# A vision tower with three attention experts on one Trainium2 core: the third expert's images shared out over both partition halves

## The chip, the cores and the metric

The kernel runs on one core of a Trainium2 chip. The time is device microseconds of one execution. It is measured without a profile; beside it one execution was profiled, and its trace is what is read below.

## The reference

16 images of 3 x 96 x 96 are cut into 36 patches each (6 x 6 of 16 x 16), so there are 576 tokens of 192 features. All arrays are float32.

```python
h = patches @ Wp.T + bp                                   # (16, 36, 768) -> (16, 36, 192)
a = window_attention(h)                                   # 12 heads of 64, window 65, zero padded
h = layernorm(h + a @ w_out + b_out)
gate = softmax(relu(h @ Wg1 + bg1) @ Wg2 + bg2)           # three experts, the two best kept
q, k = split(h @ Wqk + bqk)                               # three heads of 64, one per expert
for e in range(3):
    v = h @ Wv[e] + bv[e]
    # e == 0: q goes through a depthwise convolution of width 3 over the tokens
    # e == 1: global keys that the causal mask hides; e == 2: a position bias is added
    y[e] = causal_softmax(q[e] @ k[e].T / 8) @ v
h = layernorm(h + concat(w[e] * y[e]) @ Wp + bp)          # w: softmax over the two best gates
```

## The kernel before, in words

The images form two groups (g = 0, 1) of eight, 288 tokens each. Activations lie with the features on the partitions and the 288 tokens of a group as columns. Almost every product is made in the format float32r from a high and a low part, so that one projection is five matmuls; scores, probabilities and transposes are plain float32.

The attention runs over 16 **entries**, numbered 0 to 15: entries 0 to 5 are the six pairs of heads of group 0, 6 to 11 those of group 1, 12 and 13 the two pairs of experts of group 0, 14 and 15 those of group 1. In an entry the first head lies on partitions 0 to 63 and the second on 64 to 127. Entries 12 and 14 hold experts 0 and 1. Entries 13 and 15 hold expert 2 alone, and before the change it stands in both halves: its columns of the weights are laid out twice, and both halves compute the same for all eight images.

The work is cut into **steps**, and one list for each engine (`PE_ORDER`, `ACT_ORDER`, `DVE_ORDER`) gives their order by hand. Engines wait for one another by semaphores alone, so a step that waits holds up all that stands behind it in its list. The steps of entry n, in the order of the data:

- `qk n` (PE, L814 to L839): query and key, ten matmuls of 288 columns into two of three `proj` banks; `cq n` (ACT, L432 to L457): two copies to SBUF, three for entries 12 and 14, whose query also goes to `cn n` (DVE, L710 to L721), the convolution. The banks go round in the order of the list, and `take` makes PE wait until the bank's last user is read (`freed_by`).
- `s n` (PE, L886 to L916): the mask goes into the score bank by one matmul (L902; float32 with the position bias for entries 13 and 15, bf16 for the others), then 16 small products of 64 rows and 36 columns, one per image and half (L913). A small float32 matmul gives two records in the trace.
- `sh n` (DVE, L628 to L637): row maximum and subtraction; `ex n` (ACT, L466 to L469): exponential; `nm n` (DVE, L639 to L657): sum, reciprocal, gate's weight for entries 12 to 15, product.
- `t n` (PE, L918 to L925): three transposes, for image tiles of three, three and two images; `sp n` (ACT, L471 to L479): three copies, each with a scale of ones and zeros per partition, which spread the blocks so that images don't mix; `pv n` (PE, L927 to L946): probabilities by values, twelve records; `oh n`, `ol n` (ACT L481 to L485, DVE L659 to L663): high and low part of the output.

Around these: `xs`, `em` (splitting and embedding the patches), `wq`, `wv`, `wo`, `wf` (splitting weights; `wf 0` is the copy `ffn_hi` at L423), `v g j` and `cv g j` (values of attention), `outa`, `outb g t` (residual and output projection of a token tile), `st`, `rs`, `ap g t` (statistics on DVE, inverse deviation on ACT, normalising on DVE), `tr g` (back to features), `h1 g` (high and low part). Then the experts: `gate g` (L864 to L875), `cg g`, `lg g` (L877 to L884: sixteen products of three columns, one per image and half, at L883), `gd g` (DVE, L722 to L753: 17 small instructions), `ge g` (ACT, L522 to L528: two exponentials in the middle of `gd`, each waiting for DVE), `fv g z` and `cf g z` (experts' values), `res2`, `one2`, `out2 g t` (residual, experts 0 and 1, expert 2), `st2`, `rs2`, `ap2 g t`, `tr2 g`, `fin g` and the store. The gate's weights lie in `wgt`, per half, group, pair and image. POOL makes the low parts of weights, after a few memsets (L354 to L363).

## Time and profile before

| | us |
|---|---|
| median of the runs shown | 121.96 |
| lowest run | 121.11 |
| the profiled execution | 121.46 |
| its span, first to last instruction | 119.7 |

Three runs were timed: 121.11, 121.96 and 561.58, of which the last is an outlier. PE executes the matmuls, PEld loads their weights, DVE is the vector engine, ACT the scalar engine, POOL the third of these and SP issues the DMAs. A row of the chain that ended last has start, duration, what it was, and how many instructions were put together; a matmul's duration there is the time until the next one takes over. A row of a timeline has start, duration, engine, line, operation, operands with their shapes, and in brackets how long the engine was idle before it and what ended that. L883 is line 883. Some tiles share memory: `wqk_f` also holds the gate's values and the normalised tokens, `tw_hi` and `tw_lo` the experts' outputs, `tw_f` the result, `x_hi` and `x_lo` the attention's outputs. `g_t` and `fg_w` are `g1_t` and `fg2_w`.

### The profile page before, as it was taken

What the parts mean: (1) busy time and instruction counts of PE and PEld (TensorE: products, weight loads), DVE (VectorE), ACT (ScalarE), POOL (GpSimd) and SP (SyncE); (2) the same over time, 40 slices, a digit from 0 to 9 for tenths busy, and PEclk for the clock granted to TensorE, in tenths of its full rate; (3) what the DMA queues carried; (4) which work ended last, traced back from release to release, by engine and by line L of the source; (5) the groups of instructions that cost most, each with busy time, mean ns of one, the idle gap of its engine ahead of it and who ended that gap; (6) DMA issues with size and microseconds to landing.
All of it is one profiled execution on the core that took longest, in us unless ns stands there. A gap on an engine that the chain in (4) does not pass through costs nothing.

```text
span 119.7 us, 3567 instructions
## 1 busy us (share of the span) xinstructions
PE 109.4 (91%) x1411; PEld 97.0 (81%) x1411; DVE 76.8 (64%) x232; ACT 71.4 (60%) x196; POOL 21.5 (18%) x32
## 2 busy tenths in 40 slices
PE   6979999999999999999999899999868999897940
PEld 4769998987799888889998899899767898795930
DVE  0467848730582844593876776876847678998581
ACT  4469855459938758654458666652364485447450
POOL 6003614471400910000007900000000000000000
PEclk9999999999999999999999999999999999999998
DMA  3999999100000000000000000000000000000102
GB/s 92 255 362 404 416 424 398 43 0 5 3 0 5 3 0 0 5 0 5 0 5 0 0 0 5 0 5 0 0 3 0 8 0 5 0 5 0 54 20 74
DMA packets 3675, 7.80 MB, mean 65 GB/s; under 512 B 844, under 2 KB 1996, under 8 KB 3532
## 3 DMA queue, kind: packets, MB, share of 16 engines
q1 hardware_dynamic: 3660, 7.59, 17.6%
q8 instruction: 11, 0.18, 0.6%
q14 instruction: 4, 0.03, 0.1%
HBM read 7.14 MB, written 0.44 MB: 63 GB/s over the span
## 4 chain that ended last, share of the span: by engine, by line
PE 66%; DVE 16%; ACT 5%; issue 5%; DMA 4%; SPq 2%; DVEq 0%; ACTq 0%
PE proj L846 10%; PE score L913 8%; PE outp L944 6%; PE outp L813 4%; PE proj L831 4%; DMA x_f<-x_t 4%; PE trans L923 4%; PE proj L835 3%; PE proj L832 3%; PE score L813 3%; PE proj L838 3%; PE proj L839 3%; PE score L902 2%; PE proj L969 2%; DVE ln_st L670 2%
## 5 line engine op out<-in xcount | busy, mean ns | idle before, releaser
L478 ACT ACTIVATE pt_t<-trans,image_t 108x216 f32<-108x216 f32 (+1 forms) x48 | 16.5, 419 | 2.3 <-PE trans L923 2.3
L469 ACT ACTIVATE score<-d_t 128x296 f32<-128x296 f32 (+1 forms) x16 | 6.7, 418 | 10.8 <-DVE d_t L635 10.7
L913 PEld LDWEIGHTS score<-k_t,q_t 64*36 64x36 f32 x480 | 10.3, 111 | 3.1 <-issue 1.4
L913 PE MATMUL score<-k_t,q_t 64*36 64x37 f32 (+1 forms) x480 | 12.1, 196 | 0.1
L644 DVE TENSOR_REDUCE sm_t<-score 128x8 f32<-128x288 f32 x16 | 7.2, 449 | 7.6 <-ACT score L469 7.5
L632 DVE TENSOR_REDUCE mx_t<-score 128x8 f32<-128x296 f32 (+1 forms) x16 | 7.3, 456 | 4.5 <-PE score L913 4.4
L969 PE MATMUL proj<-wo_hi,x_hi 128*108 128x192 f32 (+1 forms) x36 | 9.5, 264 | 0.0
L971 PE MATMUL proj<-wo_lo,x_hi 128*108 128x192 f32 (+1 forms) x36 | 9.2, 256 | 0.0
L974 PE MATMUL proj<-wo_hi,x_lo 128*108 128x192 f32 (+1 forms) x36 | 9.2, 256 | 0.0
L444 ACT ACTIVATE q_t<-proj 128x288 f32<-128x288 f32 x12 | 4.9, 410 | 6.5 <-PE proj L839 6.3
L499 ACT ACTIVATE ln_ln<-ln_mv,const 108x1 f32<-108x1 f32 (+1 forms) x12 | 3.5, 294 | 8.6 <-DVE ln_mv L673 8.6
L846 PE MATMUL proj<-wv_hi,h_hi 128*108 128x384 f32 (+1 forms) x24 | 8.3, 346 | 0.0
L923 PE MATMUL trans<-const,p_t 128*108 128x128 f32 (+1 forms) x48 | 8.2, 280 | 0.0
L831 PE MATMUL proj<-h_hi,wqk_hi 128*128 128x288 f32 x24 | 7.6, 332 | 0.4 <-DVE h_lo L694 0.3
L655 DVE TENSOR_TENSOR p_t<-score,sm_t 128x288 f32<-128x288 f32 x16 | 7.3, 458 | 0.8 <-DVE sm_t L648 0.3
L635 DVE TENSOR_TENSOR d_t<-score,mx_t 128x296 f32<-128x296 f32 (+1 forms) x16 | 7.4, 464 | 0.5
L584 DVE TENSOR_TENSOR x_lo<-x_f,x_hi 128x288 fp32r<-128x288 f32 x12 | 6.1, 518 | 2.6 <-ACT x_hi L407 2.6
L485 ACT ACTIVATE x_hi<-outp 128x288 fp32r<-128x288 f32 x12 | 4.9, 409 | 4.7 <-PE outp L944 4.6
L367 POOL TENSOR_TENSOR wqk_lo<-wqk_f,wqk_hi 128x256 fp32r<-128x256 f32 x6 | 4.6, 772 | 17.1 <-ACT wqk_hi L411 17.0
L838 PE MATMUL proj<-h_lo,wqk_hi 128*128 128x288 f32 x24 | 6.7, 296 | 0.0
L839 PE MATMUL proj<-h_lo,wqk_hi 128*128 128x288 f32 x24 | 6.7, 294 | 0.0
L832 PE MATMUL proj<-h_hi,wqk_lo 128*128 128x288 f32 x24 | 6.7, 295 | 0.0
(170 smaller groups left out, 331.2 us busy)
## 6 DMA issues: line engine op xcount, KB each, us to landing
ffn_f<-f_w SPq DMA_DIRECT2D x1, 1088.0 KB, 12.6
wqk_f<-w_qk SPq DMA_DIRECT2D x2, 512.0 KB, 8.1
x_f<-x_t SPq DMA_DIRECT2D x2, 432.0 KB, 5.7
wv_f<-w_v SPq DMA_DIRECT2D x1, 768.0 KB, 6.9
wo_f<-w_out SPq DMA_DIRECT2D x1, 768.0 KB, 9.7
x_f<-x_t SPq DMA_DIRECT2D x2, 288.0 KB, 4.7
tw_f<-tok_w SPq DMA_DIRECT2D x2, 256.0 KB, 4.4
wqk_f<-w_qk SPq DMA_DIRECT2D x2, 256.0 KB, 5.0
```

The source lines that it names most:

```text
L478: nc.scalar.activation(pt_t[:, n % 2, 0:tiles, :, i], trans[0:ROWS, 0:tiles, :, 0:TOK], ACT.Copy, scale=image_t[:, i:i + 1]).then_inc(spli ...
L813: ins = nc.tensor.matmul(embed_bank[g][m][:, 0:GT], a[:, k, cols], b[:, g, k], start=(k == 0 and z == 0), stop=(k == PK - 1 and z == 2))
L831: nc.tensor.matmul(b, w_hi[:, 0, c], hcols(h_hi, g, 0), start=True, stop=False)
L832: nc.tensor.matmul(b, w_lo[:, c], hcols(h_hi, g, 0), start=False, stop=False)
L838: nc.tensor.matmul(b, w_hi[:, 0, c], hcols(h_lo, g, 0), start=False, stop=False)
L839: nc.tensor.matmul(b, w_hi[:, 1, c], hcols(h_lo, g, 1), start=False, stop=True).then_inc(projected, 1)
L846: ins = nc.tensor.matmul(out, htile(h, c, g, j), w, start=(n == 0), stop=(n == len(ops) - 1))
L913: ins = nc.tensor.matmul(s[64 * h:64 * h + TOK, im, 0:width], q, k_t[rows, n % QK_RING, im, 0:width], start=False, stop=True, skip_group_c ...
L923: ins = nc.tensor.transpose(trans[0:tile_rows(j), j].rearrange("p h s -> p (h s)"), p_t[:, n % 2, tile_cols(j)], ident)
L969: nc.tensor.matmul(b[0:rows, 0:DIM], o_hi[:, g, p, cols], wo_hi[:, p, 0:DIM], start=False, stop=False, skip_group_check=True)
L971: nc.tensor.matmul(b[0:rows, 0:DIM], o_hi[:, g, p, cols], wo_lo[:, p, 0:DIM], start=False, stop=False, skip_group_check=True)
L974: return nc.tensor.matmul(b[0:rows, 0:DIM], o_lo[:, g, p, cols], wo_hi[:, p, 0:DIM], start=False, stop=(p == PAIRS - 1), skip_group_check= ...
```

## The change

For entries 13 and 15 (`halved`) query and key now come from one projection: 128 columns of the weights, 64 of the query and 64 of the key, five matmuls into one bank. The two copies bring both to partitions 0 to 63. The eight images are shared out over the halves of the score bank in five slots: images 0 to 2 and 6 to the first half, 3 to 5 and 7 to the second, with two half-slots left empty. Maximum, exponential, sum and product run over five slots. There are two transposes, and four copies that bring the blocks to where the products with the values read them; both halves of those products read the same block. The gate's logits are computed for eight slots as before and for these five, thirteen in all; the two empty half-slots have weights of zero and a bias of -1e30 for expert 2 (`no_w`), so that their weight is zero. All three lists are ordered anew. In the diff "..." stands for what is left out: only the new arguments by which the same functions take the number of slots, and the tiles' declarations.

```diff
+HALF_SLOTS = 5
+GATES = GI + HALF_SLOTS
...
+LAST = ("ffn", 1)
+
+
+def halved(n):
+
+    return ENTRIES[n][0::2] == LAST
+
+
+def half_image(h, i):
+
+    return 3 * h + i if i < 3 else 6 + h if i == 3 + h else None
+
+
+def splits_through(n):
+
+    return sum(4 if halved(m) else 3 for m in range(n + 1))
...
 PE_ORDER = """
-em 0, em 1, em 2, em 3, em 4, em 5, em 6, qk 0, em 7, em 8, em 9, qk 1, s 0, v 0 0, s 1, em 10, em 11
-v 0 1, t 0, qk 2, v 0 2, s 2, t 1, qk 3, rows 0, s 3, pv 0, qk 4, v 1 0, t 2, qk 5, pv 1, s 4, v 1 1, pv 2
-s 5, v 1 2, t 3, qk 6, pv 3, t 4, qk 7, s 6, t 5, pv 4, s 7, qk 8, pv 5, outa 0 0, outb 0 0, t 6, s 8
-outa 0 1, outb 0 1, outa 0 2, outb 0 2, pv 6, qk 9, t 7, tr 0, s 9, qk 10, t 8, pv 7, s 10, gate 0, t 9
-qk 11, fv 0 0, s 11, t 10, pv 8, pv 9, fv 0 1, lg 0, pv 10, t 11, outa 1 0, pv 11, outa 1 1, outb 1 0
-outb 1 1, outa 1 2, outb 1 2, qk 12, tr 1, s 12, qk 13, gate 1, s 13, t 12, qk 14, lg 1, pv 12, t 13
-fv 1 0, qk 15, pv 13, s 14, s 15, fv 1 1, res2 0 0, one2 0 0, out2 0 0, res2 0 1, one2 0 1, out2 0 1, t 14
-res2 0 2, one2 0 2, out2 0 2, pv 14, t 15, tr2 0, res2 1 0, pv 15, res2 1 1, one2 1 0, one2 1 1, out2 1 0
+em 0, em 1, em 2, em 3, em 4, em 5, em 6, qk 0, em 7, s 0, qk 1, em 8, em 9, em 10, s 1, v 0 0, qk 2
+em 11, s 2, t 0, v 0 1, v 0 2, t 1, qk 3, pv 0, rows 0, s 3, t 2, qk 4, v 1 0, s 4, qk 5, v 1 1, t 3, pv 1
+s 5, pv 2, pv 3, t 4, qk 6, pv 4, qk 7, v 1 2, s 6, s 7, t 5, qk 8, pv 5, outa 0 0, s 8, outb 0 0, t 6
+outa 0 1, outb 0 1, outa 0 2, outb 0 2, qk 9, t 7, pv 6, tr 0, s 9, qk 10, pv 7, t 8, s 10, gate 0, qk 11
+t 9, pv 8, fv 0 0, pv 9, s 11, fv 0 1, t 10, lg 0, pv 10, t 11, outa 1 0, pv 11, outa 1 1, outb 1 0
+outb 1 1, outa 1 2, outb 1 2, qk 12, tr 1, s 12, qk 13, gate 1, s 13, t 12, lg 1, pv 12, qk 14, t 13
+qk 15, fv 1 0, pv 13, s 14, fv 1 1, s 15, res2 0 0, res2 0 1, one2 0 0, out2 0 0, one2 0 1, t 14, res2 0 2
+one2 0 2, out2 0 1, out2 0 2, pv 14, t 15, tr2 0, pv 15, res2 1 0, res2 1 1, one2 1 0, out2 1 0, one2 1 1
 out2 1 1, res2 1 2, one2 1 2, out2 1 2, tr2 1
 """
 ACT_ORDER = """
-xs 0, xs 1, xs 2, xs 3, xs 4, xs 5, wq 0, xs 6, xs 7, xs 8, hh 0, wq 1, xs 9, xs 10, cq 0, wv 0, cq 1
-xs 11, wq 2, ex 0, ex 1, cv 0 0, wq 3, wq 4, cv 0 1, cq 2, sp 0, cv 0 2, hh 1, wq 5, sp 1, cq 3, ex 2
-br 0, cq 4, oh 0, cv 1 0, wo 0, ex 3, oh 1, cq 5, sp 2, oh 2, ex 4, cv 1 1, cv 1 2, sp 3, cq 6, ex 5, sp 4
-oh 3, cq 7, ex 6, oh 4, sp 5, cq 8, ex 7, oh 5, sp 6, rs 0 0, rs 0 1, wf 0, rs 0 2, ex 8, cq 9, oh 6, h1 0
-sp 7, cq 10, ex 9, sp 8, cg 0, sp 9, ex 10, oh 7, cq 11, oh 8, ex 11, sp 10, oh 9, oh 10, sp 11, ge 0
-oh 11, rs 1 0, rs 1 1, rs 1 2, cq 12, h1 1, ex 12, cq 13, cg 1, ex 13, sp 12, cq 14, ge 1, sp 13, oh 12
-oh 13, cq 15, ex 14, ex 15, rs2 0 0, sp 14, rs2 0 1, rs2 0 2, sp 15, fin 0, oh 14, oh 15, rs2 1 0, rs2 1 1
-rs2 1 2, fin 1
+xs 0, xs 1, xs 2, xs 3, xs 4, xs 5, wq 0, xs 6, xs 7, xs 8, hh 0, xs 9, wq 1, xs 10, cq 0, wv 0, cq 1
+xs 11, wq 2, ex 0, wq 3, wq 4, cv 0 0, cq 2, hh 1, wq 5, wo 0, ex 1, cv 0 1, sp 0, cv 0 2, ex 2, sp 1
+cq 3, br 0, cq 4, sp 2, ex 3, cv 1 0, oh 0, cq 5, ex 4, cv 1 1, oh 1, sp 3, ex 5, oh 2, sp 4, cq 6, oh 3
+cq 7, cv 1 2, ex 6, sp 5, cq 8, oh 4, oh 5, ex 7, wf 0, sp 6, ex 8, rs 0 0, rs 0 1, rs 0 2, cq 9, h1 0
+oh 6, sp 7, cq 10, ex 9, oh 7, sp 8, cg 0, ex 10, cq 11, sp 9, oh 8, oh 9, ex 11, sp 10, oh 10, sp 11
+ge 0, oh 11, rs 1 0, rs 1 1, rs 1 2, cq 12, h1 1, ex 12, cq 13, cg 1, ex 13, sp 12, ge 1, cq 14, sp 13
+oh 12, oh 13, cq 15, ex 14, ex 15, sp 14, rs2 0 0, rs2 0 1, rs2 0 2, sp 15, oh 14, fin 0, oh 15, rs2 1 0
+rs2 1 1, rs2 1 2, fin 1
 """
 DVE_ORDER = """
-xs 0, xs 1, xs 2, xs 3, xs 4, xs 5, xs 6, hl 0, xs 7, xs 8, xs 9, wv 0, im 0, xs 10, sh 0, xs 11, sh 1
-nm 0, nm 1, hl 1, sh 2, br 0, pm 0, nm 2, sh 3, ol 0, nm 3, ol 1, sh 4, sh 5, ol 2, nm 4, nm 5, sh 6, ol 3
-nm 6, ol 4, sh 7, ol 5, st 0 0, nm 7, ap 0 0, st 0 1, sh 8, ap 0 1, st 0 2, ap 0 2, nm 8, h1 0, ol 6, sh 9
-nm 9, sh 10, nm 10, ol 7, cf 0 0, sh 11, ol 8, nm 11, cf 0 1, ol 9, ol 10, gd 0, ol 11, st 1 0, st 1 1
-ap 1 0, ap 1 1, st 1 2, ap 1 2, cn 12, h1 1, sh 12, nm 12, sh 13, nm 13, gd 1, cn 14, ol 12, ol 13, sh 14
-cf 1 0, nm 14, sh 15, st2 0 0, cf 1 1, st2 0 1, nm 15, st2 0 2, ap2 0 0, ap2 0 1, ap2 0 2, ol 14, fin 0
-ol 15, st2 1 0, st2 1 1, st2 1 2, ap2 1 0, ap2 1 1, ap2 1 2, fin 1
+xs 0, xs 1, xs 2, xs 3, xs 4, xs 5, xs 6, xs 7, hl 0, xs 8, xs 9, im 0, xs 10, sh 0, wv 0, nm 0, xs 11
+sh 1, hl 1, nm 1, sh 2, nm 2, sh 3, br 0, nm 3, sh 4, ol 0, nm 4, ol 1, sh 5, pm 0, ol 2, ol 3, nm 5, sh 6
+nm 6, ol 4, sh 7, ol 5, sh 8, nm 7, st 0 0, st 0 1, ap 0 0, ap 0 1, st 0 2, ap 0 2, nm 8, h1 0, ol 6, sh 9
+nm 9, ol 7, sh 10, nm 10, ol 8, cf 0 0, ol 9, sh 11, nm 11, cf 0 1, ol 10, gd 0, ol 11, st 1 0, st 1 1
+ap 1 0, ap 1 1, st 1 2, ap 1 2, cn 12, h1 1, sh 12, nm 12, sh 13, nm 13, gd 1, cn 14, cf 1 0, ol 12, ol 13
+sh 14, cf 1 1, sh 15, nm 14, st2 0 0, nm 15, st2 0 1, st2 0 2, ap2 0 0, ap2 0 1, ap2 0 2, fin 0, ol 14
+ol 15, st2 1 0, st2 1 1, ap2 1 0, st2 1 2, ap2 1 1, ap2 1 2, fin 1
 """
...
-            if kind == "qk":
+            if kind == "qk" and halved(key):
+                plan("q", key, (k_s, key + 1))
+            elif kind == "qk":
                 plan("q", key, (q_s, key + 1) if ENTRIES[key][0::2] != ("ffn", 0) else (taps_s, ENTRIES[key][1] + 1))
                 plan("k", key, (k_s, key + 1))
...
+            pool.memset(no_w[:], 0.0).then_inc(zeroed, 1)
+            pool.wait_ge(zeroed, 6)
+            pool.memset(no_w[32:33, 2:3], NEG).then_inc(zeroed, 1)
...
+                if halved(n):
+                    both, col = bank("q", n)[:, 0:GT], B_QK + 2 * p
+                    nc.scalar.activation(q_t[0:HD, n % QK_RING], both[0:HD], ACT.Identity,
+                                         bias=bias[0:HD, col:col + 1]).then_inc(q_s, 1)
+                    nc.scalar.activation(k_t[0:HD, n % QK_RING, :, 0:TOK], by_image(both[HD:128]), ACT.Identity,
+                                         bias=bias[HD:128, col + 1:col + 2]).then_inc(k_s, 1)
+                    return
...
-                    if p == 0:
-                        act.wait_ge(conv_b_s, 2)
-                        if g:
-                            act.wait_ge(scored, ENTRY_OF[("ffn", 0, 0)] + 1)
-                        nc.scalar.activation(qc_t[:], by_image(q[0:HD]), ACT.Identity, bias=conv_b[:],
-                                             scale=bias[0:HD, B_CONVW + 1:B_CONVW + 2]).then_inc(taps_s, 1)
+                    act.wait_ge(conv_b_s, 2)
+                    if g:
+                        act.wait_ge(scored, ENTRY_OF[("ffn", 0, 0)] + 1)
+                    nc.scalar.activation(qc_t[:], by_image(q[0:HD]), ACT.Identity, bias=conv_b[:],
+                                         scale=bias[0:HD, B_CONVW + 1:B_CONVW + 2]).then_inc(taps_s, 1)
...
+                if halved(n):
+                    for i in range(3):
+                        nc.scalar.activation(pt_t[:, n % 2, 0:2, 0, i], trans[0:ROWS, 0, :, 0:TOK], ACT.Copy,
+                                             scale=image_t[:, i:i + 1]).then_inc(split, 1)
+                    nc.scalar.activation(pt_t[0:2 * TOK, n % 2, 2, 0, 0:2], trans[0:2 * TOK, 1, :, 0:TOK],
+                                         ACT.Copy).then_inc(split, 1)
+                    return
...
-                nc.vector.tensor_tensor(d_t[:, n % 2, :, 0:width], s[:, :, 0:width],
-                                        mx_t[:, n].unsqueeze(2).broadcast_to([128, GI, width]),
+                nc.vector.tensor_tensor(d_t[:, n % 2, 0:slots, 0:width], s[:, :, 0:width],
+                                        mx_t[:, n, 0:slots].unsqueeze(2).broadcast_to([128, slots, width]),
...
-                    link(nc.vector.tensor_tensor(sm_t[:, n, 2], sm_t[:, n, 1], wgt[:, g, p], ALU.mult))
+                    link(nc.vector.tensor_tensor(share, inverse, wgt_last[:, g] if halved(n) else wgt[:, g], ALU.mult))
...
-                nc.vector.tensor_tensor(by_image(p_t[:, n % 2]), e[:, :, 0:TOK],
-                                        sm_t[:, n, 2].unsqueeze(2).broadcast_to([128, GI, TOK]),
+                nc.vector.tensor_tensor(by_image(p_t[:, n % 2, 0:slots * TOK]), e[:, :, 0:TOK],
+                                        share.unsqueeze(2).broadcast_to([128, slots, TOK]),
...
-                wide = lambda z: z.unsqueeze(2).broadcast_to([128, GI, 3])
+                wide = lambda z: z.unsqueeze(2).broadcast_to([128, GATES, 3])
                 dve.wait_ge(projected, ready[("lg", g)])
-                lg = bank("lg", g)[:, 0:3 * GI].rearrange("p (i e) -> p i e", e=3)
+                lg = bank("lg", g)[:, 0:3 * GATES].rearrange("p (i e) -> p i e", e=3)
...
+                nc.vector.tensor_tensor(wgt[0:64, g], kept[0:64, 0:GI, 0], s[4][0:64, 0:GI], ALU.mult).then_inc(gated, 1)
+                nc.vector.tensor_tensor(wgt[64:128, g], kept[64:128, 0:GI, 1], s[4][64:128, 0:GI],
+                                        ALU.mult).then_inc(gated, 1)
+                nc.vector.tensor_tensor(wgt_last[:, g], kept[:, GI:GATES, 2], s[4][:, GI:GATES],
+                                        ALU.mult).then_inc(gated, 1)
...
-                banks = [take(name, n)[:, 0:GT] for name in "qk"]
-                cols = (slice(0, 128), slice(128, 256))
+                if halved(n):
+                    banks, cols = [take("q", n)[:, 0:GT]], (slice(HD, HD + 128),)
+                else:
+                    banks = [take(name, n)[:, 0:GT] for name in "qk"]
+                    cols = (slice(0, 128), slice(128, 256))
...
+                for i in range(HALF_SLOTS):
+                    for h in range(2):
+                        im = half_image(h, i)
+                        ins = nc.tensor.matmul(b[SLOT * h:SLOT * h + SLOT, 3 * (GI + i):3 * (GI + i) + 3],
+                                               g1_t[:, im or 0], fg2_w[:] if im is not None else no_w[:],
+                                               start=True, stop=True)
                 ins.then_inc(projected, 1)
...
-                nc.tensor.matmul(s[:, :, 0:width], idn, mask.unsqueeze(1).broadcast_to([128, GI, width]), start=True,
+                nc.tensor.matmul(s[:, :, 0:width], idn, mask.unsqueeze(1).broadcast_to([128, slots, width]), start=True,
...
+                if halved(n):
+                    for i in range(HALF_SLOTS):
+                        for h in range(2):
+                            im = half_image(h, i)
+                            if im is not None:
+                                ins = nc.tensor.matmul(s[64 * h:64 * h + TOK, i, 0:width],
+                                                       q_t[0:HD, n % QK_RING, TOK * im:TOK * im + TOK],
+                                                       k_t[0:HD, n % QK_RING, im, 0:width],
+                                                       start=False, stop=True, skip_group_check=True)
+                    ins.then_inc(scored, 1)
+                    return
...
+                    pe.wait_ge(split, splits_through(n - 1))
                 pe.wait_ge(normed, n + 1)
+                if halved(n):
+                    for j, blocks in enumerate((slice(0, 3), slice(3, 5))):
+                        rows = TOK * (blocks.stop - blocks.start)
+                        ins = nc.tensor.transpose(trans[0:rows, j].rearrange("p h s -> p (h s)"),
+                                                  p_t[:, n % 2, TOK * blocks.start:TOK * blocks.stop], ident)
+                    ins.then_inc(transposed, 1)
+                    return
...
-                pe.wait_ge(split, 3 * n + 3)
+                pe.wait_ge(split, splits_through(n))
...
-                        probs = pt_t[0:rows, n % 2, j, h].rearrange("p i t -> p (i t)")[:, 0:rows]
+                        probs = pt_t[0:rows, n % 2, j, 0 if halved(n) else h].rearrange("p i t -> p (i t)")[:, 0:rows]
```

## Rows read from the trace of the kernel before

**Rows 1.** The page: busy us, share of span, instructions by engine

```profile
PE 109.4 (91%) x1411; PEld 97.0 (81%) x1411; DVE 76.8 (64%) x232; ACT 71.4 (60%) x196; POOL 21.5 (18%) x32
```

**Rows 2.** Stretches: us, busy by engine (instructions), PE clock, DMA share, GB/s

```profile
8.60:86.50 77.90, 76.97 (x1014) 69.48 (x1014) 50.53 (x149) 50.38 (x137) 19.53 (x20) 1.00 0.17 68
86.50:119.70 33.20, 25.64 (x364) 22.36 (x364) 23.37 (x77) 16.63 (x51) 0.00 (x0) 0.99 0.05 15
...
97.36:110.46 13.10, 11.71 (x170) 9.96 (x171) 11.69 (x44) 7.25 (x25) 0.00 (x0) 1.00 0.01 3
```

**Rows 3.** DVE's timeline behind 92 us

```profile
94.52 0.46 DVE L632 TENSOR_REDUCE mx_t<-score 128x8 f32<-128x288 f32 x1 [0.54 <-PE score L913]
...
97.36 0.18 DVE L729 TENSOR_REDUCE wqk_f<-proj 128x8 f32<-128x24 f32 x1
...
100.68 0.50 DVE L717 SCALAR_TENSOR_TENSOR qc_t<-q_t,bias,qc_t 64x280 f32<-64x280 f32 x1
...
102.65 0.46 DVE L632 TENSOR_REDUCE mx_t<-score 128x8 f32<-128x288 f32 x1 [0.20 <-PE score L913]
...
103.52 0.55 DVE L706 TENSOR_TENSOR wv_f<-proj,bv_all 108x384 f32<-108x384 f32 x1
...
109.23 1.23 DVE L685 TENSOR_SCALAR wqk_f<-proj,ln_mv,ln_rs 108x192 f32<-108x192 f32 x3
...
116.56 0.45 DVE L699 COPY tw_f<-proj 64x288 f32<-64x288 f32 x1 [0.44 <-PE proj L1013]
```

**Rows 4.** Chain that ended last: start us, us, what

```profile
56.98 0.33 PE trans L923 x3
...
61.66 1.91 ACT ffn_hi L423
...
76.83 1.03 PE proj L883 x32
...
92.65 0.66 PE proj L874 x5
93.31 0.49 PE score L902 x2
93.80 0.70 PE score L913 x32
...
101.86 0.77 PE score L913 x23
...
111.31 0.65 PE outp L944 x12
```

**Rows 5.** Groups by form: busy us, mean ns, idle before

```profile
L478 ACT ACTIVATE pt_t<-trans,image_t 108x216 f32<-108x216 f32 x32 | 12.2, 436 | 2.3 <-PE trans L923 2.3
...
L478 ACT ACTIVATE pt_t<-trans,image_t 108x144 f32<-108x144 f32 x16 | 6.2, 385 | 0.0
...
L685 DVE TENSOR_SCALAR wqk_f<-proj,ln_mv,ln_rs 108x192 f32<-108x192 f32 x8 | 3.6, 467 | 0.1
...
L687 DVE TENSOR_SCALAR wqk_f<-proj,ln_mv,ln_rs 108x64 f32<-108x64 f32 x4 | 1.3, 332 | 0.0
```

**Rows 6.** PE's timeline at the start of `qk 10`

```profile
66.76 0.37 PE L831 MATMUL proj<-h_hi,wqk_hi 128*128 128x288 f32 x1 [0.31 <-DVE h_lo L694]
```

**Rows 7.** ACT's timeline behind 86 us

```profile
92.89 0.49 ACT L457 ACTIVATE k_t<-proj,bias 128x288 f32<-128x288 f32 x1
...
96.77 0.51 ACT L449 ACTIVATE q_t<-proj,bias 128x288 f32<-128x288 f32 x1
...
97.62 0.50 ACT L457 ACTIVATE k_t<-proj,bias 128x288 f32<-128x288 f32 x1
...
99.14 0.22 ACT L527 ACTIVATE wqk_f<-wqk_f 128x24 f32<-128x24 f32 x1 [0.91 <-DVE wqk_f L741]
...
109.78 1.01 ACT L478 ACTIVATE pt_t<-trans,image_t 108x216 f32<-108x216 f32 x3
...
112.00 0.41 ACT L485 ACTIVATE tw_hi<-outp 128x288 fp32r<-128x288 f32 x1 [0.45 <-PE outp L944]
```

39 lines of the change are left out of this document (19 added, 20 removed).

## Prediction

> **What bounds the kernel now.** I read the page's busy shares first, then busy time by stretches, then the chain that ended last, then each engine's own timeline where the chain changes engine. PE is busy for 109.4 of 119.7 us [rows 1]. Cut at 86.5 us (where `outb 1 2`, the last matmul of group 1's attention, is done), the two parts differ. Up to there PE is busy 76.97 of 77.90 us, at full clock: what is added to PE or taken from it counts in full. After it PE is busy only 25.64 of 33.20 us; between 97.36 and 110.46 DVE is busy 11.69 of 13.10 us, and the end hangs on DVE's list [rows 2]. DVE's last copy, `fin 1`, ends at 116.56 + 0.45 = 117.0 [rows 3]; the 2.7 us from there to 119.7 are the output's way to memory. The profiled run took 121.46 us around its span of 119.7, so 1.8 us lie outside. I sum against that run. The median shown is 121.96 and the lowest 121.11, so it stands between them.
>
> **Prices on PE.** Five projection matmuls of 288 columns take 0.66 us [rows 4]. A full projection of query and key has ten, the halved one five: 0.66 us less. The mask matmul of this entry is float32 over 288 columns and takes 0.49 us, in two passes [rows 4]; over 5 x 36 = 180 columns it takes 0.49 x 180/288 = 0.31, so 0.18 less. Scores of 16 products (32 records) take 0.70 us [rows 4]; eight take 0.35, if they still overlap in pairs as now. Three transposes take 0.33 us [rows 4]; one goes, 0.11. Together 1.30 us a group. The logits, 16 products (32 records), take 1.03 us [rows 4]; ten more for the five new slots, the two empty half-slots against `no_w` included, cost 10/16 x 1.03 = 0.64 us. Net 0.66 us less PE work a group, 1.3 in all. But it doesn't fall where it is counted: `lg 0` lies in the part that PE fills, and all halved steps (entries 13 and 15) lie behind 86.5 us. So the first part gets **0.64 us longer**, and the gain has to show in the tail.
>
> The scores of a halved entry take all their operands from the same 64 rows and write to alternate halves. The nearest rows for that are two. The logits do it too, at 1.03 us for 32 records, against 0.70 for the scores [rows 4]: eight products then cost 0.52 us. The products with the values (L944) also alternate halves over one range of rows, twelve records of up to 108 columns in 0.65 us, 54 ns each [rows 4]; by the mask's 0.85 ns a column and pass (0.49/576) 108 columns alone take 92, so those pairs do overlap. Bounds 0.35 and 0.52; I take 0.35, since the logits move only three columns and must be held by something else. The Trainium skill (TensorE: Matmul & The Clock Gate, "The mechanism") says that weight loads overlap matmuls in flight only when their row groups differ; by that rule pairing would gain next to nothing and each halved entry would end 0.17 us later. The logits' row speaks for it, L944 against it.
>
> **Prices on DVE and ACT.** On DVE 192 elements take 467 ns and 64 take 332: 1.05 ns an element [rows 5]. Maximum, subtraction, sum and product go from 288 to 180 elements, 4 x 108 x 1.05 ns = 0.45 us less for each of entries 13 and 15. `gd 1`, 97.36 to 100.7 now [rows 3], grows by 15 elements in five instructions and by 5 to 10 in the rest: 0.15 us more. On ACT a split takes 436 ns for 216 elements and 385 for 144 [rows 5], so about 335 for 72, and four of these stand where there were three of about 420: no gain and no loss (bounds -0.1 to +0.2). The exponential has 108 elements less, 0.1 us; query and key remain two copies. The new memsets are on POOL, which is busy for 21.5 us of the span [rows 1], at its start: nothing; without that cover some 0.3 us.
>
> **The first part, 8.6 to 86.5.** The new lists have the same matmuls in another order, so what can be won is what PE loses now. `qk 10` starts at 66.76, after a wait of 0.31 for `h1 0` [rows 6] and a step (`s 9`) that was late itself. Behind this is the chain through the statistics of group 0, and in it the copy `wf 0`, 1.91 us of ACT between two inverse deviations [rows 4]. The new list has `wf 0` ahead of `sp 6`, where ACT has time; `rs 0 2` isn't behind it, and `ap 0 2` and `tr 0` come up to 0.9 us sooner. I laid the new lists out by hand over the durations of before, with their waits and proj banks, and got `qk 10` at 65.9. Earlier on `s 0` goes ahead of `em 8`, and `qk`, `v` and `pv` alternate so that a copy is done one step ahead; where one is late (`cv 0 2` for `qk 3`, `sp 0` for `t 1`) it costs under 0.1. Bounds for the reordering: 0 (each stall that goes is replaced) to 1.3. I take 0.85. Against the 0.64 of `lg 0` the attention of group 1 ends 0.2 us earlier.
>
> **The tail, step by step** (on the old clock). `qk 12`, `tr 1`, `s 12` stand as they were. The copies for `s 13` end at 92.89 + 0.49 = 93.38 as before [rows 7], but its mask is long done; the eight products start at 93.45 and `sh 13` at 94.0, straight behind `nm 12`, not at 94.52 [rows 3]: 0.5 won. `sh 13` and `nm 13`, 0.45 shorter, end at 96.3 instead of 97.36. Meanwhile `lg 1` goes ahead of `pv 12` and `qk 14`: from 94.4, 1.03 + 0.64 and the way through the array, ready at 96.25. So `gd 1` starts at 96.3 and ends at 99.8. Behind `qk 14` (1.33 by the row of five) `lg 1` would have set it to 97.6.
>
> Here is a wait with a queue behind it. `ge 1` now stands before `cq 14` on ACT, and its second exponential waits for DVE: it starts at 99.14, 1.8 us after `gd 1` [rows 3, 7]. Behind it stand `cq 14` (96.77 to 98.12, 1.35) and `sp 13` (1.01, as `sp 15`) [rows 7], and for these wait `fv 1 0`, `pv 13`, `s 14`. With G the start of `gd 1`, `cq 14` starts at G + 2.05, `sp 13` ends at G + 4.4, and after `pv 13` (0.65) and the mask the products of `s 14` start at G + 5.35. For G = 96.3 that is 101.65, against 101.86 now [rows 4]: of 1.0 us won 0.2 is left, as ACT is now what `s 14` waits for. DVE uses its slack: `cf 1 0` (0.55) [rows 3] is done ahead of `sh 14`. From `sh 14` (102.4, now 102.65) to the end of the three `ap2 0` (109.23 + 1.23 = 110.46) [rows 3] DVE needs 7.8 - 0.45 (entry 15) - 0.5 (`cf 1 0`) = 6.9: done at 109.3, 1.1 earlier. `st2 0 1` now stands behind `nm 15`, so `t 15` can go at 108. `sp 15` waits for `rs2 0 2` as before, 108.7 instead of 109.78; `pv 15` has no `res2 1 0` before it, and `oh 15` starts at 110.65 instead of 112.00 [rows 7]. From there the end is the old one, with `ap2 1 0` pushed ahead of `st2 1 2`, 0.1 lost: `fin 1` starts at 115.3 instead of 116.56 [rows 3], **1.25 us won** in the tail.
>
> Sum: 121.46 + 0.64 - 0.85 - 1.25 = 120.0. A layout by hand overlooks gaps such as the 0.31 of [rows 6]; with 0.2 for one, **120.2 us**.
>
> **Rivals.**
> 1. *The wait moves, little is left.* ACT's queue (`ge 1`, `cq 14`, `sp 13`) takes the tail's first gain, and new waits in the first part eat the 0.85; 0.7 of the tail remains. For it: `s 14` gains only 0.2 in my own layout. Against it: 0.45 and `cf 1 0` come off the engine that sets the end there. 121.46 + 0.64 - 0.7 = 121.4.
> 2. *More comes off.* All of the 1.3 in the first part, and `s 14` keeps the whole 1.0 because `cq 14` isn't what it waits for: 121.46 + 0.64 - 1.3 - 1.25 - 0.8 = 118.8. For it: PE is idle for 7.6 us behind 86.5 [rows 2]. Against it: the queue on ACT stands in the list.
> 3. *Slower: the gate's wait ahead of `cq 14`.* G decides: up to 96.5 the products of `s 14` start no later than now, and each 0.1 us beyond costs 0.1. If the halved scores and `lg 1` come late, so that `gd 1` starts at 97.4 as now, `s 14` starts at 102.75, 0.9 later, and DVE idles meanwhile. With nothing won in the first part: 121.46 + 0.64 + 0.9 = 123.0. Against it: `lg 1` has been taken ahead of 1.3 us of projection.
> That the change doesn't do what it says I exclude: the counts follow from the lists.
>
> **How the numbers follow.** Forecast (119.5 to 121) 0.52; rival 1 (121 to 122) 0.2; rival 2 (under 119.5) 0.17; rival 3 (over 122) 0.11. 8 in 10: 119.0 to 122.2. A measurement here tells about 2% from no change, and 2% under 121.5 to 122 is 119.1 to 119.5. Faster by over 2%: rival 2, 0.17; slower by over 2% (124 and more): the far end of rival 3, 0.04; within: 0.79.
>
> **What the next profile should show.** Halved scores of 0.35 us (0.52 if pairs don't overlap); logits of 1.67; `outb 1 2` 0.2 us earlier; `gd 1` 1.2 us earlier; an ACT wait before the second gate exponential with `cq 14` behind it; DVE without a gap from `sh 14` to `ap2 0 2`; a span of 118.3 to 118.6. I am wrong if group 1's attention ends later than now, or if the way from there to `fin 1` is less than 0.7 us shorter.

## The result, and the profile after

| | before | after |
|---|---|---|
| median, us | 121.53 (4 runs) | 122.65 (4 runs) |
| lowest | 120.99 | 121.84 |
| profiled execution | 121.46 | 123.23 |
| its span | 119.7 | 121.5 |

The change makes the kernel slower, by 0.9%: ratio 1.0088, 95% interval 1.0045 to 1.0131. Forecast was 120.2 us, 1.3 us less than before; it came out 1.1 more. The ratios here and in the table of the experiments leave out executions more than 1.5% above the fastest of their kernel, most of which have a low clock of TensorE, so the medians, over all executions, have to be read beside them.

First the stretches of the changed kernel, cut where the last matmul of group 1's attention is done (now 87.85), and one more stretch that will matter (columns as in [rows 2]):

```profile
8.60:87.85 79.25, 78.25 (x1034) 70.17 (x1034) 52.26 (x149) 51.53 (x136) 19.44 (x20) 1.00 0.17 66
87.85:121.50 33.65, 25.62 (x340) 22.48 (x340) 23.10 (x77) 16.53 (x53) 0.00 (x0) 0.91 0.05 15
98.40:101.80 3.40, 3.40 (x16) 3.34 (x15) 2.33 (x15) 1.36 (x5) 0.00 (x0) 0.50 0.02 5
```

Against [rows 2] the first part takes 79.25 us instead of 77.90, 1.35 more where 0.2 less was expected, and the second 33.65 instead of 33.20. The last row is new: for 3.4 us TensorE runs at 0.50 of its clock, at 1.2 GHz. In the profile of before the clock was at 1.00 up to 118.9 us.

PE's timeline around the first logits (mask of `s 11`, `lg 0`, `pv 10`) in the kernel before, and under it ACT's (`ex 11`, `sp 10`):

```profile
73.52 0.30 PE L902 MATMUL score<-band,bfc 128*128 128x296 bf16 x1
76.76 1.10 PE L883 MATMUL proj<-fg_w,g_t 33*64 33x3 f32 x32
77.79 0.72 PE L944 MATMUL outp<-pt_t,x_f 108*64 108x108 f32 x12
```

```profile
76.09 0.42 ACT L469 ACTIVATE score<-d_t 128x296 f32<-128x296 f32 x1
76.43 1.03 ACT L478 ACTIVATE pt_t<-trans,image_t 108x216 f32<-108x216 f32 x3
```

The same in the changed kernel:

```profile
75.58 0.30 PE L952 MATMUL score<-band,bfc 128*128 128x296 bf16 x1
77.44 1.10 PE L927 MATMUL proj<-fg_w,g_t 33*64 33x3 f32 x32
78.39 0.55 PE L932 MATMUL proj<-fg_w,g_t 33*64 33x3 f32 x13
...
79.15 0.72 PE L1012 MATMUL outp<-pt_t,x_f 108*64 108x108 f32 x12
```

```profile
77.62 0.42 ACT L500 ACTIVATE score<-d_t 128x296 f32<-128x296 f32 x1 [1.51 <-DVE d_t L673]
77.98 1.03 ACT L516 ACTIVATE pt_t<-trans,image_t 108x216 f32<-108x216 f32 x3
```

Read it backwards. `pv 10` (L944, now L1012) needs the three copies of `sp 10` (L478, now L516). They stand on ACT behind `ex 11` (L469, L500), which waits 1.51 us for DVE; DVE has `sh 11` to do for it, and that needs `s 11`. Before, `s 11`'s mask (L902) starts at 73.52 and `ex 11` at 76.09. The new PE list has `pv 8` and `pv 9` ahead of `s 11`, where they stood behind it: 75.58 and 77.62. From `lg 0` to `pv 10` there are 1.71 us instead of 1.03.

The tail, on DVE (`sh 13`, first of `gd 1`, `sh 14`, three of `ap2 0`, last of `ap2 1`, `fin 1`):

```profile
95.53 0.35 DVE L670 TENSOR_REDUCE mx_t<-score 128x5 f32<-128x180 f32 x1 [0.17 <-PE score L963]
...
97.72 0.19 DVE L768 TENSOR_REDUCE wqk_f<-proj 128x13 f32<-128x39 f32 x1
...
104.95 0.46 DVE L670 TENSOR_REDUCE mx_t<-score 128x8 f32<-128x288 f32 x1
...
110.76 1.23 DVE L724 TENSOR_SCALAR wqk_f<-proj,ln_mv,ln_rs 108x192 f32<-108x192 f32 x3
...
117.42 0.47 DVE L724 TENSOR_SCALAR wqk_f<-proj,ln_mv,ln_rs 72x192 f32<-72x192 f32 x1 [0.22 <-ACT ln_rs L541]
118.33 0.45 DVE L738 COPY tw_f<-proj 64x288 f32<-64x288 f32 x1 [0.44 <-PE proj L1081]
```

And PE's timeline from the halved scores to the end of the low stretch:

```profile
95.02 0.47 PE L963 MATMUL score<-k_t,q_t 64*36 64x36 f32 x16 [0.70 <-ACT k_t L470]
95.50 0.51 PE L991 MATMUL trans<-const,p_t 128*108 128x128 f32 x3
95.94 1.10 PE L927 MATMUL proj<-fg_w,g_t 33*64 33x3 f32 x32
96.90 0.55 PE L932 MATMUL proj<-fg_w,g_t 33*64 33x3 f32 x13
...
97.72 0.72 PE L1012 MATMUL outp<-pt_t,wv_f 108*64 108x108 f32 x12
98.37 0.59 PE L875 MATMUL proj<-h_hi,ffn_hi 128*128 128x288 f32 x1
98.76 0.44 PE L876 MATMUL proj<-h_hi,ffn_lo 128*128 128x288 f32 x1
99.00 0.44 PE L875 MATMUL proj<-h_hi,ffn_hi 128*128 128x288 f32 x1
...
102.10 0.29 PE L883 MATMUL proj<-h_lo,ffn_hi 128*128 128x288 f32 x1
```

The projection matmuls of `qk 14` (L875, L876) start every 0.24 us and last 0.44, those at 102.10 last 0.29 and start every 0.13: the low clock doubles the step. `qk 14` takes 2.55 us instead of 1.51.

`qk 0` starts anywhere from 12.36 to 13.41 us into the span in the profiles of this document, so the table below counts from the start of `qk 0` (first part) and of `qk 12` (tail).

| us | before | after |
|---|---|---|
| `qk 10` behind `qk 0` | 54.06 | 54.54 |
| `lg 0` | 64.06 | 64.76 |
| `outa 1 0` (behind `pv 10`) | 66.03 | 67.41 |
| `qk 12` | 74.02 | 75.40 |
| `gd 1` behind `qk 12` | 10.64 | 9.64 |
| mask of `s 14` | 14.58 | 15.84 |
| `pv 15` | 24.52 | 24.25 |
| `fin 1` | 29.84 | 30.25 |

So the first part lost 1.38 in three pieces, 0.48 up to `qk 10`, 0.22 to `lg 0` and 0.68 there, and `gd 1` was won as forecast, but lost again up to `s 14`.

### The profile page after: what moved, and what is told of

Its sections match the earlier page's. It is cut to its first block, busy times and chain, and to the rows that moved or that the text cites. A ratio compares the mean times of both kernels' runs of the same rounds, so it can differ in the third digit from the quotient of the medians.

```text
span 121.5 us, 3561 instructions
## 1 busy us (share of the span) xinstructions
PE 110.4 (91%) x1407; PEld 97.8 (80%) x1407; DVE 78.2 (64%) x232; ACT 72.5 (60%) x198; POOL 21.5 (18%) x34
## 4 chain that ended last, share of the span: by engine, by line
PE 74%; DVE 11%; issue 4%; ACT 4%; DMA 4%; SPq 2%; ACTq 0%; DVEq 0%
PE proj L890 12%; PE outp L1012 8%; PE score L974 7%; PE proj L875 5%; PE trans L991 4%; PE outp L854 4%; DMA x_f<-x_t 4%; PE proj L876 3%; PE proj L882 3%; PE proj L879 3%; PE proj L883 3%; PE score L854 3%; PE proj L1037 2%; DVE ln_st L709 2%; PE score L952 2%
## 5 line engine op out<-in xcount | busy, mean ns | idle before, releaser
L516 ACT ACTIVATE pt_t<-trans,image_t 108x216 f32<-108x216 f32 (+1 forms) x42 | 14.6, 423 | 1.7 <-PE trans L991 1.6
L683 DVE TENSOR_REDUCE sm_t<-score 128x8 f32<-128x288 f32 (+1 forms) x16 | 7.0, 439 | 8.6 <-ACT score L500 8.6
L500 ACT ACTIVATE score<-d_t 128x296 f32<-128x296 f32 (+2 forms) x16 | 6.6, 411 | 8.6 <-DVE d_t L673 8.6
L670 DVE TENSOR_REDUCE mx_t<-score 128x8 f32<-128x296 f32 (+2 forms) x16 | 7.1, 447 | 5.8 <-PE score L974 5.4
L974 PE MATMUL score<-k_t,q_t 64*36 64x37 f32 (+1 forms) x416 | 10.5, 196 | 0.0
L702 DVE TENSOR_TENSOR x_lo<-outp,x_hi 128x288 fp32r<-128x288 f32 x12 | 5.4, 454 | 5.2 <-ACT x_hi L523 5.2
L875 PE MATMUL proj<-h_hi,wqk_hi 128*128 128x288 f32 x24 | 7.6, 331 | 0.6 <-DVE h_lo L733 0.3
L673 DVE TENSOR_TENSOR d_t<-score,mx_t 128x296 f32<-128x296 f32 (+2 forms) x16 | 7.2, 450 | 0.6
L694 DVE TENSOR_TENSOR p_t<-score,sm_t 128x288 f32<-128x288 f32 (+1 forms) x16 | 7.1, 443 | 0.6
L392 POOL TENSOR_TENSOR ffn_lo<-ffn_f,ffn_hi 128x1088 fp32r<-128x1088 f32 x1 | 2.5, 2532 | 27.6 <-ACT ffn_hi L448 27.6
L882 PE MATMUL proj<-h_lo,wqk_hi 128*128 128x288 f32 x24 | 6.8, 299 | 0.0
L876 PE MATMUL proj<-h_hi,wqk_lo 128*128 128x288 f32 x24 | 6.7, 295 | 0.0
```

What stands on the lines that cost most here:

```text
L516: nc.scalar.activation(pt_t[:, n % 2, 0:tiles, :, i], trans[0:ROWS, 0:tiles, :, 0:TOK], ACT.Copy, scale=image_t[:, i:i + 1]).then_inc(spli ...
L875: nc.tensor.matmul(b, w_hi[:, 0, c], hcols(h_hi, g, 0), start=True, stop=False)
L876: nc.tensor.matmul(b, w_lo[:, c], hcols(h_hi, g, 0), start=False, stop=False)
L882: nc.tensor.matmul(b, w_hi[:, 0, c], hcols(h_lo, g, 0), start=False, stop=False)
L974: ins = nc.tensor.matmul(s[64 * h:64 * h + TOK, im, 0:width], q, k_t[rows, n % QK_RING, im, 0:width], start=False, stop=True, skip_group_c ...
```

## The experiments

Sixteen kernels, each timed against the kernel before in interleaved rounds. The profiled executions, from PE's and DVE's timelines, in us; "low" counts the executions with a granted clock below 0.985 in the mean, which more than 3.6 us at 1.2 GHz make. Of the 114 executions of the kernel before in these rounds none was low. A star marks profiles with a low stretch between `qk 0` and `fin 1`, called a fall below.

The mark is rough and counts too few. In every profile the clock is low once more behind `fin 1`, where TensorE has nothing left to do, for 0.1 to 2.9 us. An execution with one fall of 3.4 us and a short low end therefore comes out at 0.985 or 0.986 and isn't counted: the profiles of `old_new_nolog` and `old_new_nolog_filled` are such. In `nolog_s11_up` three executions at 0.985 took 122.6 to 122.9 us, three at 0.986 and 0.987 120.8 to 121.6.

| kernel | median | ratio, 95% interval | `qk 12` behind `qk 0` | `fin 1` behind `qk 12` | low |
|---|---|---|---|---|---|
| before | 121.5 to 121.7 | 1 | 74.02 | 29.84 | 0 of 114 |
| after | 122.65 | 1.0045 to 1.0131 | 75.40 | 30.25* | 2 of 4 |
| `old_lists` | 123.14 | 1.0073 to 1.0161 | 76.31* | 29.87 | 2 of 4 |
| `new_lists` | 126.14 | 1.0292 to 1.0404 | 76.89* | 33.09* | 3 of 4 |
| `old_then_new` | 124.3 | 1.0105 to 1.0255 | 76.27* | 30.23* | 4 of 4 |
| `no_extra_logits` | 123.41 | 1.0078 to 1.0193 | 75.47 | 30.24* | 2 of 4 |
| `old_new_nolog` | 122.25 | 0.9994 to 1.0057 | 74.24 | 30.49* | 8 of 12 |
| `old_lists_nolog` | 121.85 | 0.9975 to 1.0028 | 74.17 | 29.60 | 4 of 12 |
| `nolog_filled` | 123.76 | 1.0072 to 1.016 | 75.69 | 29.02 | 5 of 10 |
| `old_new_nolog_filled` | 121.29 | 0.9925 to 0.9985 | 74.19 | 30.50* | 4 of 12 |
| `old_math_new_tail` | 124.57 | 1.0225 to 1.029 | 74.07 | 33.65* | 4 of 6 |
| `old_new_nolog_filled2` | 121.13 | 0.9947 to 0.9994 | 74.14 | 29.13 | 0 of 12 |
| `after_filled` | 123.87 | 1.0095 to 1.0199 | 77.01* | 30.39* | 4 of 6 |
| `nolog_s11_up` | 122.67 | 0.9965 to 1.0043 | 74.64 | 29.00 | 4 of 12 |
| `filled2_wf_up` | 121.0 | 0.9926 to 0.9976 | 74.15 | 29.13 | 0 of 12 |
| `after_s11_filled` | 123.48 | none | 75.20 | 30.40* | 4 of 6 |
| `filled2_thin` | 121.14 | 0.994 to 0.9996 | 74.10 | 29.06 | 3 of 12 |
| `filled2_old_end` | 120.81 | 0.9916 to 0.9963 | 74.11 | 28.91 | 0 of 12 |

**1 to 4: order or arithmetic?** My theory was at first that three separate causes had been added up (A): the order of the first part, the extra logits, the clock. Rivals: the order is innocent (B), the halved steps bring the low clock (C).

`old_lists`: the new arithmetic, with the three lists of before.

> The new arithmetic (halved entries, thirteen gate slots) under the three old lists. Theory A (three separate causes: lg 0 costs 0.68 us in the first part, the new order of the first part costs another 0.67, and the TensorE clock falls to 1.2 GHz behind lg 1 in some executions at 1.5 us): outb 1 2 ends 0.68 us later than in the kernel before (86.55), and with qk 14 between s 13 and lg 1 the thin stretch is broken up, so no fall of the clock; 121.6 to 122.0 us. Theory B (the order is sound, and the later end of the first part comes from the arithmetic alone, which moves waits as well): outb 1 2 at 87.2 here too, 122.2 or more.

`new_lists`: the arithmetic of before, with the new lists.

> The old arithmetic under the three new lists. Theory A: the order itself costs 0.67 us before outb 1 2, which ends at 86.5, and the clock stays at 2.4 GHz since s 13, t 12 and lg 1 are followed by full projections and have no 20 extra small matmul records; 121.8 to 122.3 us. Theory B: outb 1 2 at 85.9 or earlier, and 121.0 or less.

`old_then_new`: the new arithmetic, each list old up to the end of group 1's attention, and new behind.

> The new arithmetic; each list is the old one up to the end of group 1's attention and the new one behind it. Theory A: outb 1 2 at 86.55, behind it the tail of the changed kernel, 29.6 us to the last copy where the clock stays up and 31.1 where it falls: 121.0 us in some executions, 122.5 in others. Theory B: no better than the changed kernel, 122.6.

`no_extra_logits`: the changed kernel without the ten extra products; the weights of the five slots come from the eight that were there, by four small products on DVE instead of one.

```diff
-                nc.vector.tensor_tensor(wgt_last[:, g], kept[:, GI:GATES, 2], s[4][:, GI:GATES],
-                                        ALU.mult).then_inc(gated, 1)
+                for rows, slots, ims in ((slice(0, 64), slice(0, 3), slice(0, 3)), (slice(0, 64), slice(3, 4), slice(6, 7)),
+                                         (slice(64, 128), slice(0, 3), slice(3, 6)),
+                                         (slice(64, 128), slice(4, 5), slice(7, 8))):
+                    nc.vector.tensor_tensor(wgt_last[rows, g, slots], kept[rows, ims, 2], s[4][rows, ims],
+                                            ALU.mult).then_inc(gated, 1)
```

> The changed kernel without the ten extra logits of each group: the weights of the five slots are taken from the eight slots that both halves have anyway, by four small DVE products in place of one, and the empty slots are zeroed once. Theory A (extra logits cost 0.68 in the first part and, as 20 of 52 three-column records in lg 1, let the clock fall): outb 1 2 at 86.5, gd 1 0.6 us sooner behind it, no low clock between 95 and 105 us in any execution; 120.3 to 120.8 us. Rival C (the clock falls because of the halved projections, scores and transposes): a fall as often as before at 1.5 us, 121 to 122 us.

Measured: with the old lists `qk 10` stands at 54.19, near 54.06, and with the new ones at 54.52 to 54.54 whatever the arithmetic; the same with `lg 0` (64.11 to 64.20 against 64.71 to 64.76). So the new order costs 0.65 us by `lg 0`, alone: B falls. The ten logits are the surprise. In the old order they lengthen `lg 0` to `pv 10` from 1.03 to 1.61 us; in the new order that distance is 1.71 with them, 1.72 with the old arithmetic and 1.71 without them: they lie wholly in the wait for `sp 10`. A falls as a sum; what replaces it is D: **the order costs 1.34 to 1.38 us by itself (`outa 1 0` at 67.37 in `new_lists`, 67.41 in the changed kernel), and the extra logits 0.58 only where that wait isn't.** The low clock is in the tail of three of the four profiles and behind `lg 0` in three, and at both places in `new_lists`, where no step is halved: the halved steps aren't needed for a fall, and C falls as the only cause. All four medians lie above what A had expected, by 1.1 to 3.8 us, and `new_lists` is the slowest kernel of all, with 33.09 us of tail; `old_math_new_tail` below shows why.

**5 to 8: the halved entries alone, and TensorE kept full.** All without the extra logits. `old_new_nolog` has the lists of `old_then_new`, `old_lists_nolog` those of before, `nolog_filled` is `no_extra_logits` with dummy products ahead of the waits of `pv 10` and `pv 12`, and `old_new_nolog_filled` is `old_new_nolog` with the same ahead of `pv 12`:

```diff
+                if n in (12,):
+                    for _ in range(6):
+                        nc.tensor.matmul(outp[n % 2][:, 0:256], zeros[:, 0:128], zeros[:], start=True, stop=True)
                 pe.wait_ge(split, splits_through(n))
```

> Old lists up to the end of group 1's attention, new ones behind it, and the weights of the five slots taken from the eight slots there are, so no extra logits. Theory D (the new order of the first part costs 1.35 us whatever the logits do; the extra logits cost 0.6 only in the old order; a low clock follows a stretch in which TensorE has three-column matmuls and waits): outb 1 2 at 85.9 as in the kernel before, no low clock near 80 us, a tail of 29.7 to 31.2 us with and without a fall near 98: 119.9 to 121.3 us, the lower in at least half of the executions. Rival O (the order of the first part is innocent, start and DMA scatter explain it): no clear difference from the run no_extra_logits, 123.

> All three old lists with the new arithmetic and no extra logits: the halved entries alone. Theory D: outb 1 2 at 85.9; entries 13 and 15 save about 0.5 us by the shorter DVE steps and 0.4 by qk 13, qk 15; qk 14 stands between s 13 and lg 1 and keeps TensorE filled, so the clock stays up: 120.5 to 121.0 us in all executions. Rival H (it is the halved projections, scores and transposes that let the clock fall): a fall between 95 and 110 us in a third or more of the executions, 121.5 to 122.5.

> The run no_extra_logits (new lists) with six dummy matmuls of 256 columns ahead of pv 10 and pv 12, where TensorE waits 0.8 us for ACT anyway; their output is overwritten. Theory D: no fall of the clock near 80 or 99 us in any execution, the 0.65 us of dummies hidden in the wait, 121.6 to 122.0 us. Rival E (the fall has nothing to do with how full TensorE is there): falls as often as in no_extra_logits, 122.3 to 123.8.

> The run old_new_nolog with six dummy matmuls ahead of pv 12 alone. Theory D: no fall near 98 us in any execution, and 119.9 to 120.4 us in all of them, the fastest of all versions. Rival E: some executions 1.5 us above the rest at a clock of 0.975, as in the changed kernel.

Measured: with the old first part `qk 12` is back at 74.2. `old_lists_nolog`, the halved entries in the old order, gains only 0.24 us in the tail of its profile, which has no fall. But 4 of its 12 executions were low, and they took 123.0 to 124.6 us against 121.1 to 122.2 for the other eight, while none of the 33 executions of the kernel before in the same rounds was low. That is what rival H had said: the halved steps do bring falls of their own, in the old order too. Where in the kernel, no profile shows. Where the clock stayed up (`nolog_filled`) the new tail takes 29.02, 0.82 less than before; where it fell 30.24 with the same tail, so a fall costs 1.2 us. The six dummies ahead of `pv 12` brought the low executions from 8 to 4 of 12, but not to none, and the median from 122.25 to 121.29. In `nolog_filled` half stayed low. All four medians missed what D had expected, by 0.85 to 1.8 us. The clock depends on how TensorE is filled, but six dummies don't settle it.

**9 to 12: order of the tail alone, more dummies, and `s 11`.**

`old_math_new_tail`: the arithmetic of before, old lists up to the end of group 1's attention, new ones behind.

> The arithmetic of the kernel before (eight logit slots, sixteen projection matmuls a group, whole masks and scores), its three lists up to the end of group 1's attention, and the new lists behind. Stretches with the clock at 0.5 in these profiles always stand behind a place where TensorE has just waited. Theory D: the order of the tail alone, without halved steps, puts the second group of logits and pv 12 ahead of qk 14 and leaves TensorE waiting there, so several of the executions lose 1.2 to 1.6 us to the low clock; outb 1 2 is where it was, 85.9 us into the span; gd 1 starts about 10 us behind qk 12 instead of 10.6, and the executions at full clock have a span of 119.3 to 119.9; median 0.2 us above to 0.6 below the kernel before if most are undisturbed. Rival C (it is the halved steps that bring the low clock): granted clock 0.99 or more in nearly all executions, as in the kernel before, and the median 0.6 to 1.0 us faster.

`old_new_nolog_filled2`: five dummies more, ahead of `s 13`'s mask, and seven instead of six ahead of `pv 12`.

> old_new_nolog with twelve dummy 128x256 products instead of the six of old_new_nolog_filled: five ahead of s 13's mask and seven ahead of pv 12, all in time in which TensorE waits. Theory D (the clock falls behind a thin stretch of TensorE): at most 2 of the executions show a granted clock below 0.985, against 5 of 12 with six dummies and 10 of 12 with none; median 120.5 to 121.0 us, spans 118.7 to 119.4. Rival E (the clock falls whatever TensorE does): as many low executions as with six, median 121.2 to 121.6. Should the dummies not fit into the waits, outa 1 4 comes 0.1 to 0.3 us later and the undisturbed spans are 118.9 to 119.7.

(This expectation counts the executions at 0.985 as well, hence its 5 and 10 for the table's 4 and 8.)

`after_filled`: the changed kernel, extra logits included, with five and two.

> The changed kernel whole, with five dummy 128x256 products ahead of s 13's mask and two ahead of pv 12. Theory D: the first part stays as late as in the changed kernel (outb 1 2's last step some 87.2 us into the span), the low clock goes from most executions, and the median is 121.7 to 122.2 us, 0.2 to 0.6 above the kernel before. Theory A (each part of the change costs by itself, the extra logits 0.6 us among them) gives the same number here, so this run weighs the clock alone. Rival E: half the executions stay low and the median is 122.4 to 122.9.

`nolog_s11_up`: `no_extra_logits` with `s 11` moved up, on all three engines.

```diff
-t 9, pv 8, fv 0 0, pv 9, s 11, fv 0 1
+t 9, fv 0 0, s 11, pv 8, pv 9, fv 0 1
-sp 9, oh 8, oh 9, ex 11, sp 10
+sp 9, oh 8, ex 11, oh 9, sp 10
-ol 7, sh 10, nm 10, ol 8, cf 0 0, ol 9, sh 11, nm 11, cf 0 1
+ol 7, sh 10, nm 10, cf 0 0, sh 11, ol 8, nm 11, ol 9, cf 0 1
```

> no_extra_logits with one move on each of three engines: s 11 stands ahead of pv 8 again, and with it sh 11 and ex 11 ahead of ol 8, nm 11 and oh 9. Theory D (at pv 10 the new order waits for sp 10, which stands on ACT behind ex 11, which stands behind sh 11, which waits for s 11): from lg 0 to outa 1 0 there are 2.0 to 2.1 us instead of 2.65, qk 12 starts 74.7 to 74.9 us after qk 0 instead of 75.47, and the span is 0.5 to 0.7 us shorter than no_extra_logits at the same clock (119.8 to 120.0 at full clock). Rival (pv 10 waits for sp 10's own input or something else of the order): the step pv 10 stays at 1.6 to 1.7 us and qk 12 at 75.4 to 75.6.

`nolog_s11_up` settles `pv 10`. Its ACT and PE timelines:

```profile
76.72 0.42 ACT L498 ACTIVATE score<-d_t 128x296 f32<-128x296 f32 x1
...
77.78 1.04 ACT L514 ACTIVATE pt_t<-trans,image_t 108x216 f32<-108x216 f32 x3 [0.31 <-PE trans L987]
```

```profile
77.67 1.10 PE L929 MATMUL proj<-fg_w,g_t 33*64 33x3 f32 x32
78.96 0.72 PE L1008 MATMUL outp<-pt_t,x_f 108*64 108x108 f32 x12 [0.20 <-ACT pt_t L514]
```

`ex 11` no longer waits; `sp 10` waits for its own transposes instead, and `pv 10` starts 1.29 us behind `lg 0` instead of 1.71, still more than the 1.03 of before. `lg 0` itself comes 0.4 earlier, as `s 11` up fills a gap ahead of it. `qk 12` starts at 74.64, 0.83 sooner. D holds here: of the 0.83, half is won ahead of `lg 0` and half at `pv 10`. The other 0.62 that the new order of the first part costs stay.

`old_math_new_tail` was far slower than either theory had it: 33.65 us of tail. Its timelines, DVE's (first of `gd 1`) and ACT's (second gate exponential, `cq 14`), show that the condition of rival 3 of the prediction came true, and that something else came on top:

```profile
97.08 0.17 DVE L729 TENSOR_REDUCE wqk_f<-proj 128x8 f32<-128x24 f32 x1
```

```profile
98.84 0.22 ACT L527 ACTIVATE wqk_f<-wqk_f 128x24 f32<-128x24 f32 x1 [1.07 <-DVE wqk_f L741]
100.34 0.50 ACT L449 ACTIVATE q_t<-proj,bias 128x288 f32<-128x288 f32 x1 [1.27 <-PE proj L839]
```

Without halved steps `gd 1` starts 10.55 us behind `qk 12`, hardly sooner than before, and `cq 14` starts at 13.81, where it was 10.05. The gate's exponential ends at 99.06, and ACT then idles for another 1.27 us: what ends last is the wait for `qk 14`, which the new list has behind `lg 1` and `pv 12` and which ran on the low clock here. How much of it is the order alone, no profile at full clock shows; the two executions above 0.985 took 124.19 and 124.37, still 2.7 us and more above the kernel before. So the new order of the tail only pays with the halved steps, and these pay little without it (0.24): neither half has a gain of its own. The clock was low in 4 of 6. Together with `old_lists_nolog` this says: the new order brings falls without halved steps, and halved steps bring them in the old order.

In `old_new_nolog_filled2` none of the twelve executions was low. The stretches around `lg 1` and `qk 14`, for the kernel with no dummies (`old_new_nolog`, first fence; the clock falls at its 96.55) and with twelve, each from some 1.7 us ahead of `lg 1`:

```profile
93.07:96.50 3.43, 2.16 (x52) 1.68 (x51) 2.63 (x10) 2.45 (x7) 0.00 (x0) 1.00 0.01 2
96.50:100.00 3.50, 3.39 (x21) 3.27 (x22) 2.73 (x19) 0.45 (x2) 0.00 (x0) 0.51 0.00 0
```

```profile
93.70:97.10 3.40, 3.25 (x63) 2.64 (x61) 2.60 (x10) 2.39 (x7) 0.00 (x0) 1.00 0.01 2
97.10:100.50 3.40, 3.33 (x32) 2.84 (x30) 2.63 (x19) 1.57 (x5) 0.00 (x0) 1.00 0.00 0
```

PE was busy 2.16 of 3.43 us ahead of the fall, and 3.25 of 3.40 with dummies. But `after_filled` missed, at 123.87 us: the clock fell there, and behind `lg 0` as well, where the extra logits stand and `pv 10` waits.

**13 to 16: what was open.**

`filled2_wf_up`: `old_new_nolog_filled2` with one move on ACT, `wf 0` ahead of `sp 6`. It was the heart of the 0.85 forecast for the first part.

```diff
-oh 5, sp 6, rs 0 0, rs 0 1, wf 0, rs 0 2
+oh 5, wf 0, sp 6, rs 0 0, rs 0 1, rs 0 2
```

> old_new_nolog_filled2 with one move, on ACT: wf 0 ahead of sp 6 instead of between rs 0 1 and rs 0 2, as the new list has it. By the prediction's layout ap 0 2 and tr 0 come up to 0.9 us sooner and qk 10 starts 0.3 to 0.85 us earlier, at 53.2 to 53.8 us behind qk 0 instead of 54.08. Theory D (the copy was nearly hidden, since PE is full up to there and rs 0 2 then waits for the statistics): qk 10 at 53.9 to 54.05, tr2 1 at 102.1 to 102.25 behind qk 0 instead of 102.25, and no difference in the median, 120.9 to 121.2 us.

```profile
55.32 2.01 ACT L446 ACTIVATE ffn_hi<-ffn_f 128x2176 fp32r<-128x2176 f32 x1
...
61.50 0.20 ACT L539 ACTIVATE ln_rs<-ln_ln 108x1 f32<-108x1 f32 x1
63.14 0.29 ACT L535 ACTIVATE ln_ln<-ln_mv,const 72x1 f32<-72x1 f32 x1 [1.44 <-DVE ln_mv L710]
```

```profile
64.98 0.69 PE L1083 MATMUL proj<-const,wqk_f 108*128 108x108 f32 x6
...
66.80 0.37 PE L877 MATMUL proj<-h_hi,wqk_hi 128*128 128x288 f32 x1 [0.32 <-DVE h_lo L731]
```

The copy is out of the way (55.32), yet ACT now idles for 1.44 us and the last inverse deviation (L535) starts at 63.14, waiting for DVE's statistics. `tr 0` (L1083) starts 52.23 us behind `qk 0` against 52.24 in the kernel before, because PE reaches it no sooner, and `qk 10` keeps its wait of 0.32 for the low part of `tr 0`'s own output. The copy was hidden.

`after_s11_filled`: `after_filled` with the moves of `nolog_s11_up` and two dummies ahead of `pv 10`.

> The changed kernel, with s 11, sh 11 and ex 11 moved up as in nolog_s11_up, and dummy 128x256 products: five ahead of s 13's mask, two ahead of pv 10, two ahead of pv 12. The extra logits stay. Theory D (the clock falls behind a thin stretch, and the ten extra logits are the thinnest work there is): qk 12 starts 75.1 to 75.4 us after qk 0, the extra logits showing again for 0.3 to 0.6; the falls become rarer than in after_filled (granted clock below 0.985 in 6 of its 6 profiled or timed runs but two) but do not vanish, and the median is 122.0 to 122.6 us. If waits alone bring the fall and thin matmuls have no part in it, clocks of 0.985 and more in nearly all executions, median 121.4 to 121.7.

```profile
95.10:98.50 3.40, 3.38 (x85) 2.80 (x79) 2.49 (x12) 1.70 (x6) 0.00 (x0) 1.00 0.02 5
98.50:101.90 3.40, 3.40 (x15) 3.33 (x16) 2.22 (x15) 1.39 (x4) 0.00 (x0) 0.50 0.00 0
```

PE is busy 3.38 of 3.40 us here, and the clock falls all the same, in four of six executions. The 52 records of logits (L927, L932), three columns each, take 1.6 us of that stretch. In the changed kernel itself TensorE is busy 3.27 of the 3.40 us ahead of its fall. So waits alone aren't the condition. `qk 12` comes at 75.20 against 74.64: by `pv 10` the extra logits cost 0.32 again, now that the wait is smaller, and the two dummies there another 0.32. D has that right, but its median of 122.0 to 122.6 was missed by 0.9.

`filled2_thin`: in `old_new_nolog_filled2` five of the seven dummies of 256 columns become twenty of three.

```diff
-                    for _ in range(7):
-                        nc.tensor.matmul(outp[n % 2][:, 0:256], zeros[:, 0:128], zeros[:], start=True, stop=True)
+                    for k in range(22):
+                        cols = 256 if k < 2 else 3
+                        nc.tensor.matmul(outp[n % 2][:, 0:cols], zeros[:, 0:128], zeros[:, 0:cols], start=True, stop=True)
```

> old_new_nolog_filled2 with one thing changed: of the seven dummy products ahead of pv 12, five of 256 columns are replaced by twenty of three columns, about as long together (0.6 us), where the ten extra logits stand in the changed kernel. TensorE is as full as before, but with narrow matmuls. Theory D: the low clock comes back behind pv 12, granted clock below 0.985 in four or more of 12 executions (none of 12 with wide dummies), median 121.4 to 122.2 us. Rival F (only waits bring the fall, whatever the width): at most one such execution, median 120.9 to 121.3.

Three low executions of twelve, at spans of 119.8 to 120.0 us against 118.6 in the best: between the two theories. `filled2_wf_up` and `filled2_old_end` have the same tail around `lg 1` with wide dummies, which makes none of 36 against three of 12. That points to narrow matmuls having a part in it, and twenty of them a small one: the median didn't move. It isn't shown, as the four kernels ran on four different chips, and three executions are few. (Among the 36, those at 0.985 to 0.989 took 121.1 us in the mean, as the others did, so hardly any can hide a fall.)

`filled2_old_end`: `old_new_nolog_filled2` with `ap2 1 0` behind `st2 1 2` again.

> old_new_nolog_filled2 with one move on DVE: ap2 1 0 stands behind st2 1 2 again, as in the kernel before. From pv 15 to fin 1 the new order takes 5.97 to 6.01 us in every profile against 5.32 in the kernel before. Theory G (the statistics st2 1 2 behind ap2 1 0 are what rs2 1 2 and so the last ap2 wait for): fin 1 starts 28.6 to 28.8 us after qk 12 instead of 29.13, the executions are 0.3 to 0.5 us shorter, 118.3 to 119.0 mostly, median 120.5 to 120.9 us. Rival (the loss is PE's: pv 15 no longer has res2 1 0 ahead of it, so the two residuals come behind): at most 0.1 us comes back, median 120.9 to 121.2.

DVE's end in `old_new_nolog_filled2`, then in `filled2_old_end`:

```profile
113.54 0.34 DVE L707 BATCH_NORM_STATS2 ln_st<-proj 108x6 f32<-108x192 f32 x1
...
114.61 0.35 DVE L707 BATCH_NORM_STATS2 ln_st<-proj 72x6 f32<-72x192 f32 x1
...
115.77 0.47 DVE L722 TENSOR_SCALAR wqk_f<-proj,ln_mv,ln_rs 72x192 f32<-72x192 f32 x1 [0.22 <-ACT ln_rs L539]
116.68 0.45 DVE L736 COPY tw_f<-proj 64x288 f32<-64x288 f32 x1 [0.44 <-PE proj L1083]
```

```profile
113.58 0.36 DVE L707 BATCH_NORM_STATS2 ln_st<-proj 72x6 f32<-72x192 f32 x1 [0.21 <-PE proj L1071]
...
114.08 1.23 DVE L722 TENSOR_SCALAR wqk_f<-proj,ln_mv,ln_rs 108x192 f32<-108x192 f32 x3
115.75 0.45 DVE L736 COPY tw_f<-proj 64x288 f32<-64x288 f32 x1 [0.45 <-PE proj L1083]
```

From `pv 15` to `fin 1` there are 5.79 us instead of 6.00, with 5.32 in the kernel before. So the early `ap2 1 0` explains 0.2 of the 0.7 lost there; the statistics of the last tile now wait 0.21 us for PE, whose residual products stand behind `pv 15` and no longer ahead of it. That part, some 0.5, was argued and not run. `fin 1` at 28.91 lies between what theory G and its rival had. This version has the lowest median, 120.81 us, ratio 0.9939 (0.9916 to 0.9963), though the interval overlaps those of `filled2_wf_up` and `old_new_nolog_filled2`.

## Why the prediction was wrong

**"What bounds the kernel now" held only in half.** PE does fill the first part. But from that I concluded that its small waits could be ordered away, and looked for what came late on ACT.

**The reordering, taken at 0.85 gained: the step that failed.** It cost 1.38. (a) The chain through the statistics wasn't what `qk 10` waited for; moved alone, `wf 0` gave 0.0 (`filled2_wf_up`). The wait of 0.31 [rows 6] is the way from `tr 0` to its low part, and stays whatever stands ahead. (b) My hand layout had `qk 10` at 65.9 in the span, 53.2 behind `qk 0`; it stands at 54.54. I took each step at the length it had before. `qk 0` is already 0.18 longer: its last four matmuls (L882, L883) need the low part `hl 0`, which DVE's new list has behind `xs 7`; in the changed kernel it runs from 12.68 to its last start at 14.05, before from 12.70 to 13.89. The other pieces of the 0.48 were not tried one by one. (c) The layout stopped at `qk 10`. The 0.68 at `pv 10` lay 10 us behind it: a step moved later on PE (`s 11`) held an ACT step (`ex 11`), and what queued behind that one (`sp 10`) was wanted by PE. `nolog_s11_up` gave back 0.83, 0.42 of it here.

**The lower bound of 0 for the reordering** ("each stall that goes is replaced") was therefore wrong too: a new order can lose, and the range had no room for that.

**The logits, 0.64 a group.** The size was near: 0.58 for twenty records, 29 ns each; the 32 ns that I scaled (1.03/32) held a fixed end of some 0.1 us. The place was wrong: in the new order they cost nothing, since they lie in the wait for `sp 10`. The two errors don't cancel, the wait is the dearer one.

**Prices on PE and DVE held.** The mask of 180 columns 0.33 us (0.31 expected). Halved scores take 0.43 (`s 15`) to 0.48 us (`s 13`), between my 0.35 and the 0.52 of the logits' rate. But the pairs overlap as before; here are the full scores of `s 13` in the kernel before and the halved ones in the changed kernel:

```profile
93.72 0.75 PE L913 MATMUL score<-k_t,q_t 64*36 64x36 f32 x32
```

```profile
95.02 0.47 PE L963 MATMUL score<-k_t,q_t 64*36 64x36 f32 x16 [0.70 <-ACT k_t L470]
```

One record lasts 0.20 us, so the starts of 32 are spread over 0.55 us and those of 16 over 0.27: 18 ns from record to record in both. What I scaled by half was 0.70, which holds a fixed end of some 0.15 us that doesn't shrink. So the rule that I set against it (Trainium skill, TensorE: Matmul & The Clock Gate, "The mechanism"), that weight loads run ahead only where row groups differ, isn't what this trace shows: all operands here lie in the same 64 rows and nothing was lost. The same section names the background weight buffer as a second way. DVE's instructions on 180 elements 0.35. The four splits of `sp 13` and `sp 15` take 0.84 us against 1.03 for three: 0.2 gained where I had taken nothing.

**The tail, forecast 1.25 shorter.** At full clock it is 0.82 shorter at `fin 1` (`nolog_filled`, `nolog_s11_up`, without the extra logits; with a fall the changed kernel's tail, 30.25, is that of `no_extra_logits`, 30.24), and the steps are right up to `pv 15`: `gd 1` 1.0 earlier (1.06 forecast), the mask of `s 14` where it was (14.59 against 14.58 in `nolog_s11_up`; 0.2 forecast), `pv 15` 1.5 earlier (1.35 by `oh 15`). The queue `ge 1`, `cq 14`, `sp 13` took the first gain just as written. Behind `pv 15` 0.7 is lost where I had 0.1.

**The clock was missing.** No term had it. It falls in part of the executions behind the second logits and costs 1.2 us there, more than the tail's gain. Which property of the change brings it stays open: the new order does without halved steps, and the halved steps do in the old order. The prediction told of the logits as 1.67 us of three-column matmuls, and never asked what the clock does behind them.

**The sum anew:** 121.46 + 1.38 - 0.82 = 122.0 at full clock, and 1.2 more with a fall, 123.2; measured 121.84 and 122.06 in two executions, 123.23 and 123.3 in the others. The first sign of being wrong that I named came, group 1's attention ends later; the second, a way to `fin 1` less than 0.7 us shorter, came only in executions with a fall.

**Of the rivals,** 1 (the wait moves, 121.4) was nearest in mechanism, but had its floor at "nothing won". Rival 3's condition (`gd 1` at 97.4) didn't come true in the changed kernel, and does in `old_math_new_tail`, where waiting for `qk 14` came on top. The time did land where I had put rival 3 (over 122, at 0.11), but not by its cause; that was luck.

## What to carry to other kernels

When lists are ordered by hand, lay out the whole new list, not the stretch up to the first gain, and for every step moved later ask who on the next engine waits for it and what is queued behind that one. An engine that is 99% busy has little for a new order to win and the same to lose as any. A part of a change that costs nothing may only be hiding in a wait that another part made; take both away before you judge either. A price scaled from a long row of instructions holds that row's fixed end; take the step from start to start. And watch TensorE's clock in several executions, since one profile can miss a fall.

## What the runs showed of the hardware that was not expected

- TensorE's clock fell to 1.2 GHz for 3.4 us behind a stretch in which it was busy 3.38 of 3.40 us, 1.6 of them with matmuls of three columns (`after_s11_filled`), and with dummies of 256 columns in the waits, 3.25 of 3.40 busy, none of 36 executions was low. The Trainium skill (TensorE: Matmul & The Clock Gate, "HAM oscillation — how this bites in real kernels") tells of falls through waits; the runs agree that filling the waits helps (8 low executions of 12, then 4, then none), but a fall behind 3.38 of 3.40 us isn't explained by waits.
- The same program falls or doesn't from one execution to the next, so one profile isn't enough: `old_new_nolog_filled` was profiled in one with a fall, at 122.96 us, and has a median of 121.29, below the kernel before.
- Small float32 products of 36 columns start 18 ns a record apart, whether they alternate between two halves of the rows or stay in one (fences in "Prices on PE and DVE held"); those of three columns, with 64 columns of weights, 29 ns (L927: 1.10 us for 32).
- Two copies that read partitions 0 to 63 and 64 to 127 of one bank start 0.51 us apart (`cq 13` on ACT's timeline of the changed kernel):

```profile
93.87 0.48 ACT L468 ACTIVATE q_t<-proj,bias 64x288 f32<-64x288 f32 x1
94.38 0.50 ACT L470 ACTIVATE k_t<-proj,bias 64x288 f32<-64x288 f32 x1
```

  Before, two of all 128 partitions from two banks started 0.39 apart, the second at 92.89 [rows 7]. `cq 13` is 0.13 us longer.
